# Straight-line stages, the slot transposes in the scores' bank, and the attention scores moved between the MLP tiles

## The chip, the cores and the metric

The kernel runs on one core of a Trainium2 chip. Its engines run in parallel, each with its own instruction stream in program order, and they wait for one another with semaphores: PE (TensorE, matrix products and transposes), ACT (ScalarE), DVE (VectorE), POOL (GpSimd) and SP (SyncE, which starts the DMAs). The metric is the device time of the program in microseconds.

## The reference: what is computed

Eight batch rows of 256 tokens with 256 features are normalised, and two branches are added to the input. The first is a gated slot attention with 16 heads and 64 slots:

```
A  = tril(q @ k.T) * scale                    # q, k after the rotary embedding
ok = enz * (A @ es)                           # es = exp(clip(s)), enz = 1 / cumsum(es) over tokens
qv = softmax(ok)                              # over the 64 slots
W2 = tril((qv * enz) @ es.T)
o  = W2 @ v
out = (o * rsqrt(mean(o*o) + eps) * g_norm * silu(g)) @ Wo.T
```

The second is an MLP with 2048 hidden units whose 4-bit weights are decoded on the chip: `out = (gelu(x @ Wg.T) * (x @ Wu.T)) @ Wd.T`. The result is x plus both branches, in fp32.

## The kernel before

The work is cut into 32 stages. Stage `st = 4 * hp + bp` handles pair `hp` of heads (two heads, eight pairs) and pair `bp` of batch rows (512 tokens, four pairs). With each pair of heads a stage also does one eighth of the MLP, in four tiles of 128 hidden units (`mlp_up` 0 to 3). The stages are pipelined: while a stage does its attention, PE projects v, gate, q and k for the next one (`project_vg`, `project_qk`), and it also does the output product of the one before (`outputs`).

The order on every engine is the order in which the code writes it; no scheduler moves anything. `each_stage` writes the first four stages and the last four out, and puts the 24 between them into a hardware loop of six rounds with four stages each. Each projection is three products in fp32r (high and low parts, lines 203 to 205); scores, values and transposes are plain fp32 products.

PE's order in a stage before is: `scores` for i = 0, 1 (first head, two batch rows; lines 292 and 294), `mlp_up` 0 and 1, `scores` 2 and 3 (second head), `mlp_up` 2 and 3, `gated_transpose` of the stage before (L349), `slot_scores` (L277), `project_vg` 0 and 1, `slot_reads`, `outputs` 0, `project_vg` 2, `slot_rows` (transposes of okz, L316), `outputs` 1, `project_vg` 3, the transposes of the softmax's result sm (L475), `project_qk` 0 and 1, `slot_weights` 0 (L324), `project_qk` 2 and 3, `slot_weights` 1, `values` 0, `slot_transpose` (four transposes of the next stage's es, L282) and `values` 1 (lines 338 to 341).

What surrounds these steps on the other engines:

- DVE masks each score matrix (`diagonal`, L740), and ACT copies its off-diagonal part (`off_diagonal`, L591). DVE also sums the squares of the stage before and POOL takes the power (L1092). DVE then multiplies by scale (L761) and gate (`gate_o`, L769), for which `gated_transpose` waits.
- The softmax over slots is `softmax_max` on DVE (L816), eight exponentials on ACT (`softmax_exp`, L586), the transposes L475 on PE, and `slot_query` on DVE.
- `copy_J` on ACT (L577) moves the transposed es out of its bank, for the next stage's `slot_reads`. It stands between the two squares of o (L597) at the end of a stage.
- For the next stage's q and k, `swap_halves` on ACT (L567, L568), `rope_cos` and `rope_sin` on DVE (L857, L860) and `rotate` on POOL (L1087) work in a chain with two buffers.

Two PSUM banks, `sc[0]` and `sc[1]`, hold all short-lived results of the attention. `sc_bank` gives eleven uses in a stage alternate banks, so that the roles change from stage to stage.

Of the kernel before, what the change touches and what calls it, by code (L numbers as in the profile page):

```python
# [37 lines left out]
P = 128  # L38
# [18 lines left out]
SC_SLOTS = {"A": (0, 1, 2, 3), "S": (4,), "K": (5,), "W": (6, 7, 8, 9), "E": (10,)}  # L57
SC_STEP = 11


def build(nc, x, w_qkvg, w_packed, w_scaled, w_slot, w_slot1, g_norm, rope_tab, out):
    with ExitStack() as ctx:
# [125 lines left out]
        def sc_bank(bp, kind, i=0):  # L188
            return sc[(SC_STEP * bp + SC_SLOTS[kind][i]) % 2]
# [21 lines left out]
        def _(sp):  # L211
# [12 lines left out]
            with sp.Fori(0, HP - 1) as hp:  # L224
# [15 lines left out]
        def _(pe):  # L240
# [32 lines left out]
            def slot_scores(n, bp, hp):  # L273

                if bp == 0:
                    pe.wait_ge(ws2_lo, 4 * hp + 4)
                pe.matmul(sc_bank((bp - 1) % BP, "S")[:, :] if n is not None else sc[1][:, :],  # L277
                          ws2[:, :], h1[:, bp, :], start=True, stop=True).then_inc(S_full, 1)
# [6 lines left out]
            def scores(st, bp, i, hp):  # L285
# [4 lines left out]
                dst = sc_bank(bp, "A", i)  # L290
# [20 lines left out]
            def slot_rows(st, bp):  # L311

                pe.wait_ge(okz_done, st + 1)
                dst = sc_bank(bp, "K")
# [4 lines left out]
            def slot_weights(st, bp, b):  # L319

                t0 = b * T
                pair = [(sc_bank(bp, "W", 2 * b + h), slice(h * M, (h + 1) * M)) for h in range(2)]
# [97 lines left out]
            def stage(hp, bp, first, last):  # L420
# [5 lines left out]

                for i in (0, 1):
                    if first and i == 1:
                        pe.wait_ge(clip_done, 1)
                    elif first or i == 1:  # L430
                        pe.wait_ge(J_ready, st + 1)
                    else:
                        pe.wait_ge(W_off, 4 * st)
# [29 lines left out]
                slot_rows(st, bp)  # L463
                if not first:
                    outputs(st, 1, php, st + 1)
                if not last:
# [48 lines left out]
        def _(act):  # L515
# [63 lines left out]
            def softmax_exp(st, bp):  # L579
# [3 lines left out]
                src = sc_bank(bp, "K")  # L583
# [5 lines left out]
            def off_diagonal(diag, done, dst, bp, kind, st, i, scale):  # L589
                act.wait_ge(diag, 4 * st + i + 1)  # L590
                act.activation(dst[i][:, 1, :], sc_bank(bp, kind, i)[:, P:2 * P], ACT.Copy,  # L591
# [68 lines left out]
            def stage(hp, bp, first, last):  # L660
                st = 4 * hp + bp
                npar = (bp + 1) % 2
                a_args = (A_diag, A_off, At, bp, "A", st)
                w_args = (W_diag, W_off, Wt, bp, "W", st)
                more = not (isinstance(hp, int) and hp == HP - 1)
# [28 lines left out]
                softmax_exp(st, bp)  # L694
# [24 lines left out]
                if not last:  # L719
                    copy_J(st + 1, sc_bank(bp, "E", 0)[:, :])  # L720
# [8 lines left out]
        def _(dve):  # L729
# [6 lines left out]
            def diagonal(full, done, dst, bp, kind, st, i, mask, used):  # L736
                dve.wait_ge(full, 4 * st + i + 1)
                wait(dve, *used)
                src = sc_bank(bp, kind, i)[:, 0:3 * P].rearrange("p (n t) -> p n t", n=3)
# [73 lines left out]
            def softmax_max(st, bp):  # L813
                dve.wait_ge(K_full, st + 1)
                wait(dve, p_ready, st)
                dve.tensor_reduce(mx[:, :], sc_bank(bp, "K")[:, :].rearrange("p (g m) -> p g m", m=M),  # L816
# [400 lines left out]
```

## Time and profile before

| | us |
|---|---|
| median of 3 runs | 1188.34 |
| lowest and highest | 1185.62, 1189.64 |
| profiled execution, its own time | 1186.13 |
| span of that execution | 1184.4 |
| PE busy | 1114.7 |
| DVE busy | 943.1 |
| ACT busy | 642.1 |
| POOL busy | 419.6 |

The span is the time from the first to the last instruction. Matmuls overlap in the records, so a stretch in which PE never waits is best read from start to start: 0.23 us from one full fp32r product of 512 columns to the next. The mean granted clock of PE was 0.986 of full speed. Stages begin, for instance, at 290.11 us (stage 7), 328.61 (stage 8), 362.78 (stage 9) and 397.07 (stage 10).

### The profile page before, as it was taken

The numbers are of one execution on the slowest core, as the hardware profiler recorded it, in microseconds if no ns is written. First come the engines' busy times: TensorE is split into PE (matmuls) and PEld (weight loads), VectorE is DVE, ScalarE is ACT, GpSimd is POOL, SyncE is SP. The second block draws the span as 40 slices with busy tenths as digits, with TensorE's granted clock in tenths as the row PEclk, the third lists the DMA queues.
The fourth block names the chain that finished last, engine by engine and source line by source line (L and its number), as shares of the span: only waits on it lengthen the run. The fifth ranks groups of instructions, "written<-read, shape, count | busy, mean of one in ns | idle before, by whom it ended". The sixth has DMA issues, their size and how long they took to land.

```text
span 1184.4 us, 20879 instructions
## 1 busy us (share of the span) xinstructions
PE 1114.7 (94%) x6872; PEld 941.6 (79%) x6872; DVE 943.1 (80%) x1808; ACT 642.1 (54%) x1748; POOL 419.6 (35%) x306
## 2 busy tenths in 40 slices
PE   6789999999999998999989999899998999999995
PEld 5568888888788887888878888788887888788884
DVE  6888887888868887888877888778886888877763
ACT  5355564655645565555655556464563565655451
POOL 5233242433513335232443324343251433523231
PEclk9899999999999999999999999999999999999998
DMA  4001000100001000010000100001000100000001
GB/s 157 1 1 74 1 1 1 52 22 1 1 2 73 1 1 2 1 73 1 1 3 1 74 1 1 3 16 59 1 1 2 73 1 1 1 2 19 1 19 36
DMA packets 9117, 23.19 MB, mean 20 GB/s; under 512 B 816, under 2 KB 5808, under 8 KB 7984
## 3 DMA queue, kind: packets, MB, share of 16 engines
q1 hardware_dynamic: 9008, 21.76, 5.0%
q8 instruction: 66, 1.08, 0.4%
q14 instruction: 43, 0.35, 0.1%
HBM read 19.66 MB, written 2.10 MB: 18 GB/s over the span
## 4 chain that ended last, share of the span: by engine, by line
PE 71%; issue 8%; DVE 6%; ACT 6%; POOL 3%; POOLq 0%; DVEq 0%; ACTq 0%
PE bank L203 17%; PE bank L205 16%; PE bank L204 16%; PE bank L292 5%; ACT xs L568 3%; PE bank L305 3%; PE bank L349 2%; DVE xs L860 2%; POOL qkT L1087 2%; PE bank L294 2%; DVE Wt L740 2%; ACT xs L567 2%; PE bank L282 1%; PE bank L338 1%; PE bank L341 1%
## 5 line engine op out<-in xcount | busy, mean ns | idle before, releaser
L1096 POOL TENSOR_TENSOR inter_lo<-ffb,inter_hi 128x512 fp32r<-128x512 f32 x64 | 83.3, 1323 | 433.2 <-ACT inter_hi L617 433.2
L1087 POOL TENSOR_TENSOR qkT<-ra,xs 128x512 f32<-128x512 f32 x128 | 163.5, 1277 | 95.1 <-DVE xs L860 67.6
L586 ACT ACTIVATE sm<-bank,mx 128x64 f32<-128x64 f32 x256 | 76.3, 325 | 168.5 <-DVE mx L816 168.5
L857 DVE TENSOR_TENSOR ra<-bank,rope 128x512 f32<-128x512 f32 x128 | 88.0, 687 | 55.1 <-ACT xs L568 54.9
L805 DVE RECIPROCAL enzT<-enzT 128x256 f32<-128x256 f32 x64 | 111.6, 1744 | 0.0
L860 DVE TENSOR_TENSOR xs<-xs,rope 128x512 f32<-128x512 f32 x128 | 109.0, 852 | 0.0
L203 PE MATMUL bank<-xh,wqk_hi 128*128 128x512 f32 x256 | 107.4, 420 | 0.0
L203 PE MATMUL bank<-xh,wgu_hi 128*128 128x512 f32 x256 | 106.9, 418 | 0.0
L591 ACT ACTIVATE At<-bank 128x128 f32<-128x128 f32 x128 | 35.4, 276 | 132.0 <-DVE At L740 132.0
L205 PE MATMUL bank<-xh,wgu_lo 128*128 128x512 f32 x256 | 101.6, 397 | 0.0
L203 PE MATMUL bank<-wvg_hi,xh 128*128 128x512 f32 x256 | 101.4, 396 | 0.0
L204 PE MATMUL bank<-xl,wgu_hi 128*128 128x512 f32 x256 | 101.1, 395 | 0.0
L204 PE MATMUL bank<-wvg_lo,xh 128*128 128x512 f32 x256 | 101.0, 395 | 0.0
L205 PE MATMUL bank<-wvg_hi,xl 128*128 128x512 f32 x256 | 101.0, 395 | 0.0
L205 PE MATMUL bank<-xh,wqk_lo 128*128 128x512 f32 x256 | 100.8, 394 | 0.0
L204 PE MATMUL bank<-xl,wqk_hi 128*128 128x512 f32 x256 | 100.1, 391 | 0.0
L567 ACT ACTIVATE xs<-bank 64x512 f32<-64x512 f32 x128 | 76.1, 595 | 42.8 <-POOL qkT L1087 33.7
L292 PE MATMUL bank<-qkT 128*128 128x256 f32 x256 | 79.3, 392 | 14.1 <-issue 9.7
L1092 POOL TENSOR_TENSOR rstd<-mse,mhalf 128x8 f32<-128x8 f32 x32 | 52.7, 1647 | 91.4 <-DVE mse L756 91.4
L740 DVE TENSOR_TENSOR At<-bank,mask_a 128x256 f32<-128x256 f32 x128 | 53.4, 418 | 33.8 <-PE bank L294 33.5
L203 PE MATMUL bank<-wod_hi,ogT_hi 128*128 128x256 f32 x256 | 78.8, 308 | 1.5 <-ACT ogT_hi L602 1.5
L568 ACT ACTIVATE xs<-bank 64x512 f32<-64x512 f32 x128 | 75.5, 590 | 1.5
(137 smaller groups left out, 3211.5 us busy)
## 6 DMA issues: line engine op xcount, KB each, us to landing
raw<-in_w_qkvg SPq DMA_DIRECT2D x8, 1024.0 KB, 4.9
scaled<-in_w_scaled SPq DMA_DIRECT2D x8, 640.0 KB, 7.7
packed<-in_w_packed SPq DMA_DIRECT2D x8, 384.0 KB, 5.4
acc<-in_x SPq DMA_DIRECT2D x4, 512.0 KB, 8.6
out<-acc SPq DMA_DIRECT2D x4, 512.0 KB, 3.0
ws_raw<-in_w_slot SPq DMA_DIRECT2D x8, 48.0 KB, 1.8
rope<-in_rope_tab SPq DMA_DIRECT2D x1, 256.0 KB, 7.0
osq<-in_w_slot SPq DMA_DIRECT2D x1, 128.0 KB, 3.3
```

The lines of the kernel that those rows point to most:

```text
L203: pe.matmul(dst, stat[0], mov[0], start=start, stop=False)
L204: pe.matmul(dst, stat[0], mov[1], start=False, stop=False)
L205: return pe.matmul(dst, stat[1], mov[0], start=False, stop=stop)
L292: pe.matmul(dst[:, 0:T], qkT[:, 2 * h + 1, t0:t0 + P], qkT[:, 2 * h, t0:t0 + T], start=True, stop=True)
L567: act.activation(xs[i % 2][0:64, :], pj[i][64:128, :], ACT.Copy)
L568: act.activation(xs[i % 2][64:128, :], pj[i][0:64, :], ACT.Copy).then_inc(swapped, 1)
L740: dve.tensor_tensor(dst[i][:, 0:3:2, :], src[:, 0:3:2, :], mask[:, :, :], ALU.mult).then_inc(done, 1)
L805: dve.reciprocal(enzT[par][:, c], enzT[par][:, c]).then_inc(enz_ready, 1)
L857: dve.tensor_tensor(two(ra[i % 2][:, :]), two(pj[i][:, :]), cos, ALU.mult).then_inc(cos_done, 1)
L860: dve.tensor_tensor(two(xs[i % 2][:, :]), two(xs[i % 2][:, :]), sin, ALU.mult).then_inc(sin_done, 1)
L1087: pool.tensor_tensor(qkT[:, i, :], ra[i % 2][:, :], xs[i % 2][:, :], ALU.add).then_inc(roped, 1)
L1096: pool.tensor_tensor(inter[1][e][:, :], ffb[e][:, :], inter[0][e][:, :].bitcast(F32), ALU.subtract).then_inc(inter_lo, 1)
```

## The change

It has four parts.

1. All 32 stages are written out; the hardware loop goes on every engine that had it.
2. `sc_bank` goes. Scores and weights use `sc[0]` for the one of a pair and `sc[1]` for the other, the slot scores S and the es transposes use `sc[0]`, and the okz transposes use `sc[1]`, in every stage.
3. `slot_transpose` moves on PE from between the two `values` to between `outputs` 1 and `project_vg` 3. `copy_J` moves on ACT from behind the first square of o to ahead of `softmax_exp`. `slot_weights` 0 now waits for `copy_J`.
4. On PE `scores` 0 and 1 move behind `mlp_up` 0, and `scores` 2 and 3 behind `mlp_up` 2.

```diff
         def each_stage(eng, stage):
-            for bp in range(BP):
-                stage(0, bp, bp == 0, False)
-            with eng.Fori(1, HP - 1) as hp:
-                for bp in range(BP):
-                    stage(hp, bp, False, False)
-            for bp in range(BP):
-                stage(HP - 1, bp, False, bp == BP - 1)
+            for hp in range(HP):
+                for bp in range(BP):
+                    stage(hp, bp, hp == bp == 0, hp == HP - 1 and bp == BP - 1)
...
+                mlp_up(st, bp, hp, 0)
                 for i in (0, 1):
...
                     scores(st, bp, i, hp)
-                mlp_up(st, bp, hp, 0)
                 mlp_up(st, bp, hp, 1)
+                mlp_up(st, bp, hp, 2)
                 for i in (2, 3):
                     pe.wait_ge(A_off, 4 * st + i - 1)
                     scores(st, bp, i, hp)
-                mlp_up(st, bp, hp, 2)
                 mlp_up(st, bp, hp, 3)
...
                     outputs(st, 1, php, st + 1)
+                if not last:
+                    pe.wait_ge(es_ready, st + 2)
+                    slot_transpose(sc[0], esT[nbp % 2])
                 if not last:
                     project_vg(st + 1, nbp, nhp, 3, True)
...
                 pe.wait_ge(qe_ready, st + 1)
-                pe.wait_ge(A_off, 4 * st + 4)
-                if not last:
-                    pe.wait_ge(clip_done, st + 2)
+                if not last:
+                    pe.wait_ge(J_ready, st + 2)
                 slot_weights(st, bp, 0)
...
                 values(st, bp, 0)
-                if not last:
-                    pe.wait_ge(es_ready, st + 2)
-                    pe.wait_ge(W_off, 4 * st + 3)
-                    slot_transpose(sc_bank(bp, "E", 0), esT[nbp % 2])
...
# ScalarE
-                softmax_exp(st, bp)
+                if not last:
+                    copy_J(st + 1, sc[0][:, :])
+                softmax_exp(st)
...
                 square_o(st, 0)
-                if not last:
-                    copy_J(st + 1, sc_bank(bp, "E", 0)[:, :])
                 square_o(st, 1)
```

The next rows are the instruction order as the two programs issue it; the square brackets name the semaphores that a row waits for. First PE, ahead of the transposes of sm, before: the last `project_vg` tile (wvg) stands directly behind `outputs` 1 (wod).

```order
L205 MATMUL bank<-wod_hi,inter_lo 128x256
L203 MATMUL bank<-wvg_hi,xh 128x512 [waits inter_done]
L204 MATMUL bank<-wvg_lo,xh 128x512
L205 MATMUL bank<-wvg_hi,xl 128x512
L203 MATMUL bank<-wvg_hi,xh 128x512
L204 MATMUL bank<-wvg_lo,xh 128x512
L205 MATMUL bank<-wvg_hi,xl 128x512
L475 MATMUL bank<-ident,sm 128x128 [waits acc_done,p_ready]
```

The same place after the change, where the es transposes stand between them (L273 is L282 of before, and L467 is L475):

```order
L196 MATMUL bank<-wod_hi,inter_lo 128x256
L273 MATMUL bank<-ident,esT 128x128 [waits es_ready]
L273 MATMUL bank<-ident,esT 128x128 x3
L194 MATMUL bank<-wvg_hi,xh 128x512 [waits inter_done]
L195 MATMUL bank<-wvg_lo,xh 128x512
L196 MATMUL bank<-wvg_hi,xl 128x512
L194 MATMUL bank<-wvg_hi,xh 128x512
L195 MATMUL bank<-wvg_lo,xh 128x512
L196 MATMUL bank<-wvg_hi,xl 128x512
L467 MATMUL bank<-ident,sm 128x128 [waits acc_done,p_ready]
```

Four transposes have come in between, and the transposes of sm still wait for the exponentials (p_ready). Second ACT, in the middle of a stage, before: the exponentials of the softmax follow the first two copies of v and tanh of the gate.

```order
L559 ACTIVATE vS<-bank 128x256 [waits vg_full]
L561 ACTIVATE th<-bank 128x256 [waits G_ready]
L586 ACTIVATE sm,ssum<-bank,mx 128x64 [waits rs_done,pT_full,mx_done]
L586 ACTIVATE sm,ssum<-bank,mx 128x64 x7
L559 ACTIVATE vS<-bank 128x256 [waits vg_full]
```

The same place after the change, with the copy of the transposed es to esJ (`copy_J`):

```order
L546 ACTIVATE vS<-bank 128x256 [waits vg_full]
L548 ACTIVATE th<-bank 128x256 [waits G_ready]
L564 ACTIVATE esJ<-bank 128x512 [waits ok_full,E_full]
L573 ACTIVATE sm,ssum<-bank,mx 128x64 [waits rs_done,pT_full,mx_done]
L573 ACTIVATE sm,ssum<-bank,mx 128x64 x7
L546 ACTIVATE vS<-bank 128x256 [waits vg_full]
```

The exponentials now stand behind a copy that waits for the es transposes on PE (E_full). Third PE, at the end of a stage and the start of the next, before (the six products of values 0 stand ahead of these rows):

```order
L282 MATMUL bank<-ident,esT 128x128 [waits W_off,es_ready]
L282 MATMUL bank<-ident,esT 128x128 x3
L338 MATMUL bank<-vS,Wt 128x128 [waits W_off]
L340 MATMUL bank<-vS,Wt 128x128
L341 MATMUL bank<-vS,Wt 128x128
L338 MATMUL bank<-vS,Wt 128x128
L340 MATMUL bank<-vS,Wt 128x128
L341 MATMUL bank<-vS,Wt 128x128
L292 MATMUL bank<-qkT 128x256 [waits roped,W_off]
L294 MATMUL bank<-qkT 128x128
L292 MATMUL bank<-qkT 128x256 [waits J_ready]
L294 MATMUL bank<-qkT 128x128
```

The same place after the change (L332 is L341, and L283 is L292; wgu is the MLP tile):

```order
L329 MATMUL bank<-vS,Wt 128x128 [waits W_off]
...
L332 MATMUL bank<-vS,Wt 128x128
L194 MATMUL bank<-xh,wgu_hi 128x512 [waits cos_done,w_lo]
L195 MATMUL bank<-xl,wgu_hi 128x512
L196 MATMUL bank<-xh,wgu_lo 128x512
L194 MATMUL bank<-xh,wgu_hi 128x512
L195 MATMUL bank<-xl,wgu_hi 128x512
L196 MATMUL bank<-xh,wgu_lo 128x512
L283 MATMUL bank<-qkT 128x256 [waits roped,W_off]
L285 MATMUL bank<-qkT 128x128
L283 MATMUL bank<-qkT 128x256 [waits W_off]
L285 MATMUL bank<-qkT 128x128
```

The es transposes are gone from here, values 1 keeps its own wait for W_off, and one MLP tile now stands between the values and the first scores.

## Rows read from the trace of the kernel before

**Rows 1.** Page, part 1: busy us (share of the span) xinstructions.

```profile
PE 1114.7 (94%) x6872; PEld 941.6 (79%) x6872; DVE 943.1 (80%) x1808; ACT 642.1 (54%) x1748; POOL 419.6 (35%) x306
```

**Rows 2.** Waits of PE: waiting line, releaser, us in total, times, longest us.

```profile
PE bank L282 <- ACT Wt L591: 20.2, 27, 2.1
...
PE bank L292 <- issue: 9.7, 5, 2.5
```

**Rows 3.** Windows, the five fourth stages before a jump back (span, busy, PEclk).

```profile
290.11:328.61 38.50, 35.56 (x215) 30.09 (x214) 30.83 (x56) 23.39 (x59) 19.74 (x13) 0.96 0.01 2
...
sum 192.00, PE 171.77 PEld 144.78 DVE 154.09 ACT 116.91 POOL 98.65; mean PE 34.35 PEld 28.96 DVE 30.82 ACT 23.38 POOL 19.73
```

**Rows 4.** Windows: stages 8, 16, 27 (left by the loop's end), 28 (written out).

```profile
328.61:362.78 34.17, 33.98 (x213) 28.81 (x214) 26.58 (x53) 17.82 (x51) 8.82 (x7) 1.00 0.01 2
610.46:646.25 35.79, 35.60 (x214) 30.05 (x214) 26.68 (x53) 17.82 (x51) 8.82 (x7) 0.95 0.01 2
998.01:1033.99 35.98, 33.88 (x216) 28.70 (x215) 30.80 (x56) 22.78 (x58) 18.98 (x13) 1.00 0.00 1
1033.99:1068.30 34.31, 33.89 (x216) 28.70 (x214) 27.03 (x53) 18.41 (x52) 9.58 (x8) 1.00 0.01 2
```

**Rows 5.** Timeline, softmax of stage 8: start us, us, engine, line, tiles.

```profile
347.92 0.31 ACT L586 ACTIVATE sm<-bank,mx 128x64 f32<-128x64 f32 x1 [6.36 <-DVE mx L816]
...
349.84 0.40 PE L203 MATMUL bank<-wvg_hi,xh 128*128 128x512 f32 x1
...
351.23 0.60 PE L475 MATMUL bank<-ident,sm 128*128 128x128 f32 x4
...
351.58 0.47 PE L203 MATMUL bank<-xh,wqk_hi 128*128 128x512 f32 x1
...
353.25 0.59 ACT L567 ACTIVATE xs<-bank 64x512 f32<-64x512 f32 x1
```

**Rows 6.** Timeline, softmax of stage 0.

```profile
60.85 0.31 ACT L586 ACTIVATE sm<-bank,mx 128x64 f32<-128x64 f32 x1 [3.68 <-DVE mx L816]
...
63.38 0.66 PE L475 MATMUL bank<-ident,sm 128*128 128x128 f32 x4 [2.55 <-ACT sm L586]
...
65.48 0.59 ACT L567 ACTIVATE xs<-bank 64x512 f32<-64x512 f32 x1
```

**Rows 7.** Timeline, es transposes and their copy at the end of stage 8.

```profile
360.55 0.45 ACT L591 ACTIVATE Wt<-bank 128x128 f32<-128x128 f32 x2
...
360.97 0.63 PE L282 MATMUL bank<-ident,esT 128*128 128x128 f32 x4 [0.19 <-ACT Wt L591]
...
361.64 0.60 ACT L577 ACTIVATE esJ<-bank 128x512 f32<-128x512 f32 x1 [0.15 <-PE bank L282]
```

**Rows 8.** Timeline, end of stage 7 (a fourth stage).

```profile
320.60 2.35 POOL L1066 TENSOR_TENSOR wgu_lo<-raw,wgu_hi 128x1024 fp32r<-128x1024 f32 x1
...
321.03 2.47 DVE L860 TENSOR_TENSOR xs<-xs,rope 128x512 f32<-128x512 f32 x1
...
324.29 0.95 PE L282 MATMUL bank<-ident,esT 128*128 128x128 f32 x4 [2.12 <-ACT Wt L591]
```

**Rows 9.** Timeline, starts of stages 9 and 10 up to the gated transposes.

```profile
362.78 0.60 PE L292 MATMUL bank<-qkT 128*128 128x256 f32 x2
...
363.64 0.42 DVE L740 TENSOR_TENSOR At<-bank,mask_a 128x256 f32<-128x256 f32 x1 [1.19 <-PE bank L294]
...
367.03 0.69 DVE L761 TENSOR_TENSOR scal<-rstd,rs 128x8 f32<-128x8 f32 x1
...
370.94 0.60 PE L349 MATMUL bank<-ident,og 128*128 128x128 f32 x4
...
398.28 0.41 DVE L740 TENSOR_TENSOR At<-bank,mask_a 128x256 f32<-128x256 f32 x1
...
403.24 1.12 DVE L769 SCALAR_TENSOR_TENSOR og<-bank,scal,G 128x128 f32<-128x128 f32 x4
```

**Rows 10.** Timeline, the decoding step behind `slot_query` in stage 9.

```profile
387.25 1.23 DVE L867 TENSOR_SCALAR packed<-packed 128x768 int32<-128x768 int32 x1
```

More of the change, by code:

```diff
@@ L223, in _ @@
                     sp.dma_start(scaled[:, :], w_scaled[0]).then_inc(scaled_in, 16)
-            with sp.Fori(0, HP - 1) as hp:
+            for hp in range(HP - 1):
                 sp.wait_ge(w_lo, 4 * hp + 4)
@@ L276, in slot_scores @@
                     pe.wait_ge(ws2_lo, 4 * hp + 4)
[L277 removed]
+                pe.matmul(sc[0][:, :] if n is not None else sc[1][:, :],
                           ws2[:, :], h1[:, bp, :], start=True, stop=True).then_inc(S_full, 1)
@@ L321, in slot_weights @@
                 t0 = b * T
-                pair = [(sc_bank(bp, "W", 2 * b + h), slice(h * M, (h + 1) * M)) for h in range(2)]
+                pair = [(sc[h], slice(h * M, (h + 1) * M)) for h in range(2)]
                 for dst, g in pair:
@@ L424, in stage @@
                 php = hp - 1 if bp == 0 else hp
+                mlp_up(st, bp, hp, 0)
                 for i in (0, 1):
[L428 to L431, printed above, removed]
+                    if first:
+                        pe.wait_ge(clip_done if i == 1 else J_ready, 1)
                     else:
-                        pe.wait_ge(W_off, 4 * st)
+                        pe.wait_ge(W_off, 4 * st - 1 + i)
                     scores(st, bp, i, hp)
-                mlp_up(st, bp, hp, 0)
                 mlp_up(st, bp, hp, 1)
+                mlp_up(st, bp, hp, 2)
                 for i in (2, 3):
@@ L587, in softmax_exp, with off_diagonal @@
                 ins.then_inc(p_ready, 1)
-            def off_diagonal(diag, done, dst, bp, kind, st, i, scale):
+            def off_diagonal(diag, done, dst, st, i, scale):
                 act.wait_ge(diag, 4 * st + i + 1)
-                act.activation(dst[i][:, 1, :], sc_bank(bp, kind, i)[:, P:2 * P], ACT.Copy,
+                act.activation(dst[i][:, 1, :], sc[i % 2][:, P:2 * P], ACT.Copy,
                                scale=scale).then_inc(done, 1)
@@ L662, in stage @@
                 npar = (bp + 1) % 2
-                a_args = (A_diag, A_off, At, bp, "A", st)
-                w_args = (W_diag, W_off, Wt, bp, "W", st)
-                more = not (isinstance(hp, int) and hp == HP - 1)
+                a_args = (A_diag, A_off, At, st)
+                w_args = (W_diag, W_off, Wt, st)
+                more = hp < HP - 1
                 off_diagonal(*a_args, 0, SCALE)
@@ L734, in two, with diagonal @@
                 return ap.rearrange("p (b t) -> p b t", b=2)
-            def diagonal(full, done, dst, bp, kind, st, i, mask, used):
+            def diagonal(full, done, dst, st, i, mask, used):
                 dve.wait_ge(full, 4 * st + i + 1)
                 wait(dve, *used)
-                src = sc_bank(bp, kind, i)[:, 0:3 * P].rearrange("p (n t) -> p n t", n=3)
+                src = sc[i % 2][:, 0:3 * P].rearrange("p (n t) -> p n t", n=3)
                 dve.tensor_tensor(dst[i][:, 0:3:2, :], src[:, 0:3:2, :], mask[:, :, :], ALU.mult).then_inc(done, 1)
@@ L946, in stage @@
                 par, npar, pbp = bp % 2, (bp + 1) % 2, (bp - 1) % BP
-                more = not (isinstance(hp, int) and hp == HP - 1)
-                a_args = (A_full, A_diag, At, bp, "A", st)
-                w_args = (W_full, W_diag, Wt, bp, "W", st)
+                more = hp < HP - 1
+                a_args = (A_full, A_diag, At, st)
+                w_args = (W_full, W_diag, Wt, st)
                 if bp == 3 and more:
@@ L1135, in stage @@
                 st = 4 * hp + bp
-                more = not (isinstance(hp, int) and hp == HP - 1)
+                more = hp < HP - 1
                 if first:
```

24 lines of the change are left out of this document (10 added, 14 removed).

## The prediction

> **What bounds the kernel now.** I read the page first. PE is busy for 94% of the span and the next engine, DVE, for 80% [rows 1]. So PE's own order is the clock of the kernel, and other engines matter only where PE waits. The chain that ended last says the same. The waits of PE come next. Apart from the start and the end of the program, only two groups count: 20.2 us ahead of the es transposes, where PE waits for ACT's copy of the masked weights, and 9.7 us ahead of the first scores, five times, with no releaser that the profile shows [rows 2]. The five times are the five jumps back of the loop. The windows by stage show what they cost: the fourth stages ahead of a jump last 192.0 us together [rows 3], the one that leaves the loop without a jump 35.98 us [rows 4]. The reader is to see two more things there. A stage in the loop and a written-out one take the same time (34.17 and 34.31 us, granted clock 1.00), so the loop costs nothing between its jumps. And a stage with a stretch at 1.2 GHz instead of 2.4 GHz (granted clock 0.95) takes 35.79 us instead of 34.17, which is 1.62 us more [rows 4].
>
> **1. Written-out stages: a gain of 15.3 us.** Five fourth stages give back 192.0 - 5 x 35.98 = 12.1 us. Two of the stages behind a jump were lengthened by the slow clock that its wait left behind, 2 x 1.62 = 3.2 us (one of the two is in [rows 4]). The sum is 15.3 us, of which 9.7 us is the wait itself [rows 2]. The Trainium skill ("Runtime: NRT & Kernel Launch", "Instruction fetch mechanics") states that prefetch of instructions is sequential and that a taken branch to a page that isn't held stalls the engine until it is fetched. The trace agrees, since the wait stands only at the jumps. By that rule the gain is whole; if the 9.7 us had another source that stays, the time would be some 15 us above my sum.
>
> **2. The copy ahead of the exponentials: a new wait of 2.0 us in each stage.** This is the term that decides. Call e the start of the es transposes in their new place, which is where `project_vg` 3 started before (349.84). PE then needs 0.35 us for four transposes (as L475, 351.23 to 351.58), 1.39 us for `project_vg` 3 (349.84 to 351.23), and 0.07 us more for its first product, since one behind a plain fp32 product takes 0.47 us instead of 0.40 [rows 5]. It stands before the transposes of sm at e + 1.8. ACT can start `copy_J` 0.67 us after the first es transpose (360.97 to 361.64), and it takes 0.60 us [rows 7], so the exponentials start at e + 1.28. Before, they started at 347.92, when DVE's maximum came, 1.9 us ahead of e; so their input now lies ready for 3.2 us. From the first exponential to the transposes of sm there are 2.53 us, as stage 0 shows, where PE really waited for them [rows 6]. So PE goes on at e + 3.8 instead of e + 1.8. That is 1.99 us of waiting. The slack that hid the exponentials before was 351.23 - (347.92 + 2.53) = 0.78 us, and they are moved by 3.2 us against `outputs` 1. The whole difference lies on PE's path, since there is no other instruction for PE to take. Thirty stages have both `outputs` 1 and a next stage: 30 x 1.99 = 59.7 us. Behind that wait ACT has its two copies of v, two tanh and two splits before `swap_halves`: it started 2.02 us after L475 before (351.23 to 353.25) and 2.10 us where PE had waited (63.38 to 65.48) [rows 5, 6]. So 0.08 us is lost there, and nothing is caught up.
>
> **3. The scores behind an MLP tile: a wait for the gate of 0.2 to 0.7 us.** `gated_transpose` started 8.16 us after the stage did (362.78 to 370.94). DVE's first mask came 0.86 us after the first score [rows 9]. Now the first score comes 1.46 us later (one MLP tile, 1.39 + 0.07), so the mask starts at 2.32. DVE does the sum of squares, the norm and the gate in that order behind it, and ends 6.08 us after it started (398.28 to 403.24 + 1.12) [rows 9]: 8.40 us. PE arrives at 8.16 + 0.07 = 8.23, the 0.07 being one more change from fp32 to fp32r. That makes 0.2 us of waiting in second-batch-pair and later stages, a little more (0.3) in first ones. In the second stage of each four, the multiplication by scale, an operation on eight columns, takes 0.69 us beside POOL's decoding [rows 9]; I add 0.5 us for it, which gives 0.7 us. Seven first stages at 0.3, eight second at 0.7, eight third and seven fourth at 0.2 make 10.7 us, and the last stage, which has no projections to fill the time, 1.5 us: 12.2 us. Bounds: nothing, if DVE finds the same waits elsewhere shorter, and 1.46 us x 31 = 45 us, if all of the shift showed; the rows speak for the low part.
>
> **4. The wait ahead of the es transposes doesn't go with them.** `values` 1 has a wait of its own, for the second of the two copies of which the es transposes waited for the first. The two end 0.17 us apart (0.45 us for two of 0.28) [rows 7]. So PE waits at `values` 1 for what it waited for at L282, and 0.17 us longer, and 0.08 us longer by the lateness in part 2. In the second stages the decoding step of 1.23 us [rows 10] stands on DVE between `slot_query` and the rotary part. What follows the exponentials comes 0.78 us later against PE (the slack of part 2 that is gone), and so does this step; I take it that 0.2 us of that is absorbed: 0.6 us more. Per four stages this is 4 x 0.25 + 0.6 = 1.6 us, over 7.75 fours 12.4 us. The wait of 2.12 us in fourth stages stays: DVE's `rope_sin` there takes 2.47 us beside POOL's split of the MLP weights and ends 0.55 us after it [rows 8]. The Trainium skill ("SBUF — State Buffer", "SBUF: two separate sides") states that VectorE and GpSimd share one port pair under an exclusive lock, and that the later one is blocked for the whole instruction. The rows agree; by that rule the wait can't be had by moving PE's transposes.
>
> **5. Small terms.** The es transposes cost PE 0.42 us in the new place (0.35 + 0.07), and about as much before; with the change from fp32 at the stage's start (0.07) I count 0.05 us a stage, 1.6 us. The banks' new roles add the wait of `slot_weights` 0 for `copy_J`, which ends at e + 1.3, while `slot_weights` 0 comes behind two projections more; nothing. `copy_J` no longer stands between the squares of o; ACT is idle there, so nothing is gained. The DMAs keep their places.
>
> **6. The clock.** Of the five jumps, each with two waits near 2 us within five us, three left a stretch at 1.2 GHz (granted clock 0.96 and 0.95 [rows 3, 4], and once more like the latter). That is 3 of 10 waits. Thirty new waits of 2.0 us would give 9 such stretches of 1.62 us, 14.6 us; about a third comes back, since the later wait at `values` 1 gets shorter where PE is slower ahead of it. I take 9 us. The bounds are 0 and 30 x 1.62 = 49 us.
>
> **Sum.** 59.7 + 12.2 + 12.4 + 1.6 + 9 - 15.3 = 79.6 us. The rows come from an execution of 1186.1 us in its own time, span 1184.4, which lies 2.2 us below the median of the runs. 1188.3 + 79.6 gives **1268 us**.
>
> **The rivals.**
> - Only the wait for the exponentials shows; the gate and the values' waits come out as before, and the clock stays at full speed. 1188.3 + 59.7 + 1.6 - 15.3 = 1234 us. For it: DVE and ACT idle for a fifth and more of the span [rows 1], and some of it may be in the right place. Against it: the chain of part 3 has 8.16 - 0.86 - 6.08 = 1.2 us of slack and is moved by 1.46. Chance 0.17.
> - The slow clock comes after nearly every new wait: 1268 - 9 + 49 = 1308 us. For it: the waits are as long as those that led to it. Against it: seven in ten of those didn't. Chance 0.14.
> - The other side: the exponentials are not late. They would be hidden if the path from the first es transpose to their end fitted in 1.8 us instead of 3.8, or if their input came that late already. Then parts 2 and 6 fall away, and if PE's wait of 20.2 us also went with the transposes, the time would be 1188.3 - 20.2 - 15.3 + 1.6 = 1154 us. The point that decides is e + 1.8. Every piece of the 3.8 us is a row, so I give this 0.03.
> - Writing the stages out costs elsewhere: the longer program is fetched once in place of a loop. Stages 28 to 31 are such code already and 28 shows no wait but that at L282 [rows 4]. The gain of part 1 would be lost: 1268 + 15 = 1283 us. Chance 0.05.
> - The forecast itself, within 1248 to 1288: 0.6. The last 0.01 is for no change.
>
> **Range and chances.** From between the first rival and the forecast up to between the forecast and the second: 1240 to 1296 us. A measurement here can tell about 0.3%, that is 4 us. Faster than that 0.04, within it 0.01, slower 0.95.
>
> **What the profile after would show.** Right: a wait of PE of about 2.0 us at L467 for ACT's exponentials (L573), some thirty times, 60 us in total; a wait of 0.2 to 0.7 us at L340 for DVE; a wait at the first product of the second `values` (L329) for ACT, 0.4 us in most stages and 2.3 in fourth ones; no wait without a releaser at the stage starts; stages of some 37 us and fourth ones near 39. Wrong: exponentials that start before the es transposes, or no wait at L467. If the waits are as told and the time is not, the clock's stretches are miscounted, which the windows would show.

## The result and the profile after

The changed kernel takes 1262.81 us (median of 4 runs, 1262.2 to 1263.69) against 1186.98 us before (1185.38 to 1189.64). The ratio is 1.0637, with a 95% interval of 1.0613 to 1.0661. It is slower by 6.4%. The prediction said 1268 us, with a range of 1240 to 1296 us: the median is inside the range and 5 us below the forecast. The profiled execution has a span of 1261.9 us, 77.5 us more than before.

First the page of the kernel after, its busy times (to compare with [rows 1]):

```profile
PE 1136.9 (90%) x6872; PEld 943.2 (75%) x6872; DVE 942.1 (75%) x1808; ACT 629.6 (50%) x1748; POOL 421.0 (33%) x306
```

The numbers of instructions on the engines are the same, and PE is busy for a smaller share. So the time went into PE's waits. Its waits by releaser, of the kernel after (total us, times, longest; to compare with [rows 2]):

```profile
PE bank L467 <- ACT sm L573: 52.4, 32, 2.1
PE bank L329 <- ACT Wt L578: 26.4, 30, 2.7
...
PE bank L340 <- DVE og L756: 10.6, 10, 5.9
PE bank L194 <- POOL wgu_lo L1053: 5.4, 1, 5.4
```

The five waits at the jumps are gone. The wait for the exponentials stands first, with 32 times, and the wait for ACT's copies of the weights has not gone with the es transposes: it was 20.2 us at L282 and is 26.4 us at the second `values`. The page's list understates such waits, since the modelled end of a matmul reaches over the start of the idle time. What PE really loses is better read from start to start. The timeline of stage 9 after, at the moved transposes (to compare with [rows 5]):

```profile
406.20 0.60 PE L307 MATMUL bank<-ident,okz 128*128 128x128 f32 x4
406.83 0.69 DVE L803 TENSOR_REDUCE mx<-bank 128x8 f32<-128x512 f32 x1 [0.80 <-PE bank L307]
...
409.47 0.60 PE L273 MATMUL bank<-ident,esT 128*128 128x128 f32 x4
...
410.11 0.60 ACT L564 ACTIVATE esJ<-bank 128x512 f32<-128x512 f32 x1 [8.32 <-PE bank L273]
410.60 0.31 ACT L573 ACTIVATE sm<-bank,mx 128x64 f32<-128x64 f32 x1
...
413.13 0.66 PE L467 MATMUL bank<-ident,sm 128*128 128x128 f32 x4 [1.66 <-ACT sm L573]
```

DVE has the maximum at 407.52. ACT has been idle for 8.32 us and does not start the exponentials, because `copy_J` stands ahead of them and waits for transposes that PE issues at 409.47. From there 0.64 us go by to the copy, 0.49 us to the first exponential, 2.53 us to the transposes of sm: 3.66 us, of which PE fills 1.82. It loses 1.84 us, in every one of 30 stages (3.66 us from L273 to L467 in each of them).

The windows of four stages after (stages 8 to 11: span, busy, granted clock; to compare with [rows 4]):

```profile
349.64:387.46 37.82, 35.77 (x216) 29.60 (x215) 26.67 (x53) 17.88 (x52) 9.20 (x8) 0.96 0.00 1
387.46:424.72 37.26, 34.43 (x216) 28.58 (x215) 28.07 (x56) 18.83 (x53) 13.39 (x11) 1.00 0.16 58
424.72:461.14 36.42, 34.41 (x217) 28.58 (x215) 28.79 (x57) 18.07 (x53) 9.31 (x8) 1.00 0.00 1
461.14:499.93 38.79, 34.72 (x216) 28.85 (x215) 30.89 (x57) 22.38 (x58) 19.56 (x13) 0.99 0.01 1
sum 150.29, PE 139.34 PEld 115.61 DVE 114.43 ACT 77.16 POOL 51.46; mean PE 34.84 PEld 28.90 DVE 28.61 ACT 19.29 POOL 12.86
```

The same four stages took 140.69 us before (328.61 to 469.30), so four stages have grown by 9.6 us, although the 2.1 us that the jump at 469.30 cost are gone. Around the start of each first stage of a four (here at 349.64) lies a stretch at 1.2 GHz. The timeline of the kernel after around one, the end of stage 11, shows where it begins:

```profile
498.29 0.49 PE L329 MATMUL bank<-vS,Wt 128*128 128x128 f32 x2 [2.38 <-ACT Wt L578]
...
499.06 0.39 PE L329 MATMUL bank<-vS,Wt 128*128 128x128 f32 x2
...
499.64 0.63 PE L332 MATMUL bank<-vS,Wt 128*128 128x128 f32 x2
499.93 0.77 PE L194 MATMUL bank<-xh,wgu_hi 128*128 128x512 f32 x1
500.50 0.63 PE L195 MATMUL bank<-xl,wgu_hi 128*128 128x512 f32 x1
```

PE waits 2.4 us at the second `values`, starts at full speed, and 1.1 us later the clock falls: each product then takes 0.43 us from start to start instead of 0.23. This comes after each of the seven such waits of fourth stages, and after none of the thirty waits for the exponentials. Before there were four such stretches between the first stage and the last, two after waits of fourth stages and two after jumps.

The gate's wait at `gated_transpose` is the third one. (Its longest, 5.9 us, is that of the last stage, which was there before with 6.0 us.) Stage 9 after, the second of a four, on PE (to compare with [rows 9]):

```profile
395.49 0.40 PE L196 MATMUL bank<-xh,wgu_lo 128*128 128x512 f32 x1
396.44 1.09 PE L340 MATMUL bank<-ident,og 128*128 128x128 f32 x8 [0.55 <-DVE og L756]
```

And stage 10, the third:

```profile
432.73 0.40 PE L196 MATMUL bank<-xh,wgu_lo 128*128 128x512 f32 x1
433.18 1.09 PE L340 MATMUL bank<-ident,og 128*128 128x128 f32 x8
```

The next instruction would start 0.23 us after the last one, so PE loses 0.72 us in the second stage of a four, and 0.22 us in the third, where the list of waits has nothing at all. In the first and the fourth it loses 0.24 and 0.20 us by the same reading: 1.4 us in four stages.

### The profile page after: what moved, and what is told of

Its sections match the earlier page's. It is cut to its first block, busy times and chain, and to the rows that moved or that the text cites. A ratio compares the mean times of both kernels' runs of the same rounds, so it can differ in the third digit from the quotient of the medians.

```text
span 1261.9 us, 19839 instructions
## 1 busy us (share of the span) xinstructions
PE 1136.9 (90%) x6872; PEld 943.2 (75%) x6872; DVE 942.1 (75%) x1808; ACT 629.6 (50%) x1748; POOL 421.0 (33%) x306
## 4 chain that ended last, share of the span: by engine, by line
PE 46%; ACT 17%; issue 14%; DVE 13%; POOL 4%; POOLq 0%; DVEq 0%; ACTq 0%
PE bank L194 11%; PE bank L195 10%; PE bank L196 10%; ACT sm L573 6%; DVE Wt L727 3%; DVE og L756 3%; POOL rstd L1079 3%; PE bank L340 3%; ACT xs L554 3%; ACT xs L555 3%; PE bank L296 2%; DVE xs L847 2%; ACT inter_hi L604 2%; PE bank L283 2%; DVE ra L844 1%
## 5 line engine op out<-in xcount | busy, mean ns | idle before, releaser
L777 DVE SCALAR_TENSOR_TENSOR G<-th,bank 128x256 f32<-128x256 f32 x128 | 52.4, 410 | 110.6 <-ACT th L548 110.6
L564 ACT ACTIVATE esJ<-bank 128x512 f32<-128x512 f32 x32 | 19.2, 599 | 220.0 <-PE bank L273 219.9
L194 PE MATMUL bank<-xh,wgu_hi 128*128 128x512 f32 x256 | 112.9, 441 | 5.4 <-POOL wgu_lo L1053 5.4
L847 DVE TENSOR_TENSOR xs<-xs,rope 128x512 f32<-128x512 f32 x128 | 112.0, 875 | 0.0
L196 PE MATMUL bank<-xh,wgu_lo 128*128 128x512 f32 x256 | 104.3, 408 | 0.0
L194 PE MATMUL bank<-wvg_hi,xh 128*128 128x512 f32 x256 | 104.3, 408 | 0.0
L195 PE MATMUL bank<-xl,wgu_hi 128*128 128x512 f32 x256 | 103.9, 406 | 0.0
L554 ACT ACTIVATE xs<-bank 64x512 f32<-64x512 f32 x128 | 76.3, 596 | 40.8 <-POOL qkT L1074 34.0
L329 PE MATMUL bank<-vS,Wt 128*128 128x128 f32 x256 | 57.3, 307 | 27.5 <-ACT Wt L578 26.4
```

The source lines that it names most:

```text
L194: pe.matmul(dst, stat[0], mov[0], start=start, stop=False)
L195: pe.matmul(dst, stat[0], mov[1], start=False, stop=False)
L196: return pe.matmul(dst, stat[1], mov[0], start=False, stop=stop)
L554: act.activation(xs[i % 2][0:64, :], pj[i][64:128, :], ACT.Copy)
L847: dve.tensor_tensor(two(xs[i % 2][:, :]), two(xs[i % 2][:, :]), sin, ALU.mult).then_inc(sin_done, 1)
```

## The experiments

Twelve kernels ran, in three groups of four; each was timed against the kernel before (1186.7 to 1186.8 us in these groups). Spans, waits and stretches are those of one profiled execution of each. "Slow stretches" are those at 1.2 GHz between the starts of stage 1 and stage 31. Their number can differ between executions of one kernel: the mean granted clock of the kernel before was 0.978 to 0.986, that of the changed kernel 0.979 to 0.982.

### First group: one part undone, or one part alone

**copy_behind_exp.** The changed kernel, with the copy behind the exponentials:

```diff
-                if not last:
-                    copy_J(st + 1, sc[0][:, :])
                 softmax_exp(st)
+                if not last:
+                    copy_J(st + 1, sc[0][:, :])
```

> The changed kernel with one edit: the copy of the transposed es stands behind the eight exponentials on ACT; the transposes on PE keep their new place. Theory (the exponentials wait for the copy, the copy for PE): they start again when DVE's maximum comes, PE's wait for them, 1.84 us in each of 30 stages, goes, and 55 us come back: 1208 us (1200 to 1216). Rival (the loss comes from the scores' place or from the banks' roles): above 1250 us, and the wait of PE for the exponentials turns up as another wait.

Measured: 1198.98 us, ratio 1.0097 (1.0079 to 1.0116); span 1197.5 us. Its waits of PE:

```profile
PE bank L329 <- ACT Wt L578: 23.0, 30, 2.5
...
PE bank L467 <- ACT sm L573: 2.6, 2, 2.1
```

Of 32 waits for the exponentials two are left, those of the first and the last stage. 64 us came back with two lines moved. That is more than the 55 us of the waits: there are three slow stretches instead of seven, 4 x 1.62 = 6.5 us, and the waits at L329 are 3.4 us less. The expectation (1200 to 1216 us) had counted the waits alone and was just missed.

**es_ahead_of_outputs.** The changed kernel, with the es transposes ahead of `outputs` 1 on PE and the copy left where the change put it:

```diff
                 slot_rows(st)
+                if not last:
+                    pe.wait_ge(es_ready, st + 2)
+                    slot_transpose(sc[0], esT[nbp % 2])
                 if not first:
                     outputs(st, 1, php, st + 1)
-                if not last:
-                    pe.wait_ge(es_ready, st + 2)
-                    slot_transpose(sc[0], esT[nbp % 2])
```

> The changed kernel with the es transposes directly behind the okz transposes on PE, ahead of the output product; the copy stays ahead of the exponentials on ACT. The copy can then start 1.0 us behind the first okz transpose and the exponentials 1.5 us behind it, where DVE's maximum came 1.4 us behind it before. Theory (what costs is only that the copy waits for transposes behind the output product): as with the copy behind the exponentials, 1208 us (1200 to 1216). Rival (the copy ahead of the exponentials costs its own 0.6 us of PE time wherever it waits): 1226 us.

Measured: 1199.91 us, ratio 1.0104 (1.0085 to 1.0123); span 1198.3, with four slow stretches. Here, too, only two of the waits for the exponentials are left:

```profile
PE bank L467 <- ACT sm L573: 2.6, 2, 2.1
```

The two cures are worth the same. So neither place brings the wait by itself: the copy may stand ahead of the exponentials if the transposes come early, and the transposes may come late if the copy stands behind. Only the pair costs the 1.84 us a stage. (The late transposes have a smaller price of their own; see halves_es_moved.)

**loop_out_only.** The kernel before with `each_stage` and SP's loop written out as in the change, nothing else.

> The kernel before with only the loop written out on all engines. Theory (the jumps cost 12.1 us and leave the slow clock twice): 1187 - 15.3 = 1172 us (1168 to 1177), no wait without a releaser at the stages' starts, and the waits at the es transposes as before, 20 us. Rival (the wait at the jumps has another source, or the longer program costs as much): 1187 us.

Measured: 1182.79 us, ratio 0.9965 (0.9952 to 0.9979). It is faster, by 4 us and not by 15. The waits at the jumps are gone, as expected. But the windows over the slow stretches in this kernel's trace show seven of them instead of four, one after each wait of fourth stages (three of the seven rows):

```profile
186.50:189.90 3.40, 3.35 (x16) 3.38 (x17) 1.81 (x3) 1.32 (x3) 1.94 (x2) 0.52 0.01 2
326.40:329.80 3.40, 3.40 (x17) 3.40 (x18) 1.75 (x3) 1.26 (x3) 1.88 (x2) 0.53 0.00 0
...
1026.10:1029.50 3.40, 3.40 (x18) 3.31 (x18) 1.61 (x3) 1.34 (x4) 1.72 (x2) 0.54 0.00 0
```

The sum is 12.1 us back, 3 x 1.62 = 4.9 us lost, 2.3 us lost ahead of stage 1 (see the last section), and 1.6 us lost in the last stage, where slow stretches also lie: 3.3 us back, which is the difference of the spans (1184.4 and 1181.1). The medians differ by 4.0.

The 12.1 us are the right total and the wrong parts. They were read from fourth stages [rows 3], and stage 7 among these took its 38.50 us with a wait of only 1.1 us at the jump and 1.4 us of slow clock. From start to start the five waits at the jumps add up to 10.6 us. Against loop_out_only, PE's waits at the es transposes inside the loop are 1.4 us longer, about 0.08 us each in first, third and fourth stages. So the loop did cost a little between its jumps.

My expectation (1168 to 1177 us) had the slow clock as a debt of the jumps alone. It isn't: the wait of 2 us in fourth stages, which the loop had as well, can bring it.

**scores_back.** The changed kernel with both pairs of scores back in their old places.

```diff
-                mlp_up(st, bp, hp, 0)
                 for i in (0, 1):
...
+                mlp_up(st, bp, hp, 0)
                 mlp_up(st, bp, hp, 1)
-                mlp_up(st, bp, hp, 2)
                 for i in (2, 3):
...
+                mlp_up(st, bp, hp, 2)
                 mlp_up(st, bp, hp, 3)
```

> The changed kernel with the scores back in their old places, ahead of MLP tiles 0 and 2. Theory: the waits of PE for the gate (0.2 to 0.7 us a stage, 11 us in all), one change of precision a stage (about 2 us) and 2 us in stage 0 go: 1248 us (1242 to 1254), with the wait for the exponentials still at 1.84 us a stage. Rival (the scores' place costs nothing, the loss is all of the exponentials): 1262 us. Rival (most of the loss is of the scores): below 1225 us.

Measured: 1238.96 us, ratio 1.0443 (1.0421 to 1.0465); span 1236.5. PE's waits for the gate are gone but for the last:

```profile
PE bank L467 <- ACT sm L573: 52.0, 32, 2.1
PE bank L329 <- ACT Wt L578: 26.3, 30, 2.7
...
PE bank L340 <- DVE og L756: 6.0, 1, 6.0
```

The span is 25.4 us shorter than the changed kernel's, 10 us more than expected. There is one slow stretch here instead of seven, which is 6 x 1.62 = 9.7 us. What is left for the scores' place is 15.7 us. The waits of fourth stages are as long as in the changed kernel (2.38 us in both lists), and here six of the seven did not bring the slow clock.

### Second group: the clock, the sum, and a larger dose

**two_undone.** The changed kernel with both of the edits above, copy_behind_exp and scores_back.

> The changed kernel with two edits undone: the scores stand where they stood, and the copy of es follows the exponentials on ACT. What is left of the change is the written-out stages, the banks' new roles and the es transposes ahead of the last value projection. Theory (the two edits make up the loss, and their costs add): the span of the kernel with the copy behind, 1197.5 us with three stretches of slow clock of 1.62 us, less 15.7 us for the scores, is 1177 us with none and 1188 us with seven. Rival (the costs overlap): 1195 us or more.

Measured: 1183.23 us, ratio 0.9971 (0.9961 to 0.9981); span 1181.6, with three slow stretches. 1177 + 3 x 1.62 is 1181.9. The costs add.

**split_in_halves.** The kernel of loop_out_only, and on POOL:

```diff
+            def split_half(hp, k):
+                if k == 0:
+                    pool.wait_ge(w_hi, 4 * hp + W_GU + 1)
+                ins = pool.tensor_tensor(wgu[1][:, k, :], mlp_raw[:, k, :], wgu[0][:, k, :].bitcast(F32), ALU.subtract)
+                if k == 1:
+                    ins.then_inc(w_lo, 1)
...
-                        if i == 1 and bp == 3 and more:
-                            split_lo(hp + 1, W_GU)
+                        if i in (1, 2) and bp == 3 and more:
+                            split_half(hp + 1, i - 1)
```

> The kernel before with the loop written out, and POOL's split of the MLP weights cut into two halves, one behind the second rotation and one behind the third, so that DVE's sine product in fourth stages waits for one half only. Theory (the 2 us wait of PE in fourth stages comes from that product, held up by POOL, and this wait brings the slow clock seven times): the wait falls from 2.0 to about 0.9 us, 7.7 us come back, and with the seven slow stretches 11 us more: 1182.8 - 19 = 1164 us. Rival (the wait has another cause): 1183 us. Rival (the wait falls but the slow clock stays): 1175 us.

Measured: 1162.5 us, ratio 0.9791 (0.9776 to 0.9807). The end of stage 7 in this kernel's timeline (to compare with [rows 8]):

```profile
321.50 1.28 POOL L1067 TENSOR_TENSOR wgu_lo<-raw,wgu_hi 128x512 fp32r<-128x512 f32 x1
...
321.94 1.38 DVE L856 TENSOR_TENSOR xs<-xs,rope 128x512 f32<-128x512 f32 x1
...
324.12 0.63 PE L278 MATMUL bank<-ident,esT 128*128 128x128 f32 x4 [0.96 <-ACT Wt L587]
```

DVE's sine product takes 1.38 us instead of 2.47, PE's wait is 0.96 instead of 2.02 us, and no slow stretch is left between the first stage and the last. 7 x 1.06 + 7 x 1.62 = 18.8 us; the span is 19.6 us shorter (1161.5 against 1181.1 in loop_out_only).

**split_halves_in_loop.** The same cut in the kernel before, with its loop.

> The same cut of POOL's split in the kernel before, with its loop kept. Theory: 7.7 us of waiting come back and up to 4 slow stretches (6.5 us), the jumps stay: 1186.8 - 8 to - 14 = 1173 to 1179 us; and the written-out kernel with the same cut is 10 to 12 us below this one. Rival (written-out stages gain nothing once the clock is out of the way): both within 3 us.

Measured: 1177.07 us, ratio 0.9919 (0.99 to 0.9938); span 1174.0, one slow stretch, which begins during a wait at a jump. With the clock nearly out of the way, the written-out stages are worth 14.6 us between the medians of this kernel and the last one, 12.5 us between the spans (10 to 12 us were expected). The list of waits names POOL's rotation as the releaser of the waits at the jumps here (five of the six in this row; the other, of 4.0 us, is in stage 0):

```profile
PE bank L292 <- POOL qkT L1094: 14.7, 6, 4.0
```

The five are 2.0 to 2.3 us each, where the kernel before had 0.8 to 2.5 us. The second rotation, for which PE waits there, is long done (behind stage 11 at 457.37, where PE goes on at 464.15), so I read them as the same waits. That a jump makes PE wait is shown, since the waits go with the loop; what PE waits for at a jump no run shows.

**second_copy.** The changed kernel, with one more copy on ACT ahead of `copy_J`'s, from the same bank into a tile `pad` that nobody reads.

```diff
                 wait(act, ok_full, n)
+                if n > 0:
+                    wait(act, pad_done, n - 1)
+                    act.activation(pad[:, :], src, ACT.Copy).then_inc(pad_done, 1)
                 act.activation(esJ[:, :, :].rearrange("p n m -> p (n m)"), src, ACT.Copy).then_inc(J_ready, 1)
```

> The changed kernel with one more copy of 512 columns on ACT ahead of the copy of es, into a tile that nobody reads. Theory (ACT's chain from the es transposes to the exponentials is PE's path): each of 30 stages gets 0.61 us longer at the wait for the exponentials, 18 us, before what the clock does: 1281 us, or 1270 to 1295 with the clock's changes. Rival (some other limit sets the stage's length): 1263 us.

Measured: 1291.52 us, ratio 1.0885 (1.0865 to 1.0906); span 1289.4. Its waits of PE:

```profile
PE bank L469 <- ACT sm L578: 66.6, 32, 2.1
PE bank L331 <- ACT Wt L583: 24.1, 28, 2.5
```

Each wait for the exponentials grew by 0.47 us (from 1.66 to 2.13 in the list), 30 x 0.47 = 14.1 us; two copies in a row take that, not the 0.61 us that I used. There are fourteen slow stretches instead of seven, and 7 x 1.62 = 11.3 us. Together 25.4 of the 27.5 us; the rest was not followed up. The seven new stretches come after the waits for the exponentials, now 2.3 us from start to start.

### Third group: each part on ground without slow stretches

The first three put parts of the change, or all of it, into the kernel of split_in_halves (span 1161.5), so that the clock does not blur them. In all three no slow stretch is left between stages 1 and 31.

**halves_scores_moved.** That kernel with the two pairs of scores moved as in the change.

> The written-out kernel with POOL's split in halves (1162.5 us, no slow stretch between the first and the last stage), and in it the scores' move alone. Theory (the move costs PE's waits for the gate, 1.4 us in four stages, a change of precision in each, and 2 to 3 us in stage 0): 1162.5 + 11 + 2 + 2 = 1177 us (1172 to 1181). Rival (15 us was the slow clock's doing): 1164 us.

Measured: 1185.13 us, ratio 0.9987 (0.9974 to 1.0001); span 1181.9, so 20.4 us for the move, 5 us more than expected. Its waits:

```profile
PE bank L345 <- DVE og L765: 10.6, 10, 6.0
PE bank L278 <- ACT Wt L587: 9.4, 14, 0.9
PE bank L199 <- POOL wgu_lo L1062: 6.2, 1, 6.2
...
PE bank L199 <- POOL wgu_lo L1067: 2.7, 7, 0.4
```

The last row is a wait that the two edits make together: with an MLP tile at the head of a stage, PE needs the second half of the split at once, 0.55 us from start to start, 7 times: 4 us. Without it the move costs 16.5 us, as scores_back showed from the other side (15.7). The waits for the gate are 11 to 12 us of that. The rest is about 0.07 us a stage for one more change between fp32 and fp32r, and a longer stage 0 (POOL's split at L199, 6.2 us).

**halves_es_moved.** That kernel with the new roles of the banks and the es transposes in their new place, the copy behind the exponentials.

> The written-out kernel with POOL's split in halves, the banks' new roles and the es transposes in their new place, with the copy behind the exponentials and the scores in their old places. Theory (what is left of the change costs little; PE waits at the second values for the second copy instead of the first): 1162.5 + 7 = 1169.5 us (1166 to 1173). Rival (banks and transposes are free): 1162.5 us.

Measured: 1168.37 us, ratio 0.9841 (0.9812 to 0.9869); span 1167.8. What is left of the change costs 6.3 us:

```profile
PE bank L329 <- ACT Wt L578: 15.2, 30, 1.2
```

It was 9.6 us in 14 waits at the es transposes. PE comes to the second `values` a little earlier, needs the second copy instead of the first, and waits. The new roles of the banks and the new place of the transposes were not tried apart, so the 6.3 us are for both.

**halves_whole_change.** The changed kernel with the split in halves.

> The changed kernel with POOL's split in halves. Theory (the slow clock in it follows the wait of fourth stages only, seven times, and never the wait of 1.84 us for the exponentials): the wait of fourth stages gets 1.1 us shorter, 7.5 us, and seven slow stretches go, 11.3 us: 1262.8 - 19 = 1244 us. Rival (the slow clock moves to the waits for the exponentials): 1255 us or more.

Measured: 1251.65 us, ratio 1.0549 (1.0517 to 1.0582); span 1247.2. Its waits for the exponentials and for the split's second half:

```profile
PE bank L467 <- ACT sm L573: 52.1, 32, 2.1
...
PE bank L194 <- POOL wgu_lo L1058: 3.5, 7, 0.5
```

The waits for the exponentials are the same, and no slow stretch follows any of them, so the rival is refuted for this execution. The 14.7 us that came back between the spans are the 18.8 us of split_in_halves, less 4 to 5 us of waiting for the second half, which the expectation (1244 us) had left out. The profiled execution is the fastest of the four; between the medians 11.2 us came back.

On this ground, without slow stretches, the whole change costs 1247.2 - 1161.5 = 85.7 us: 20.4 for the scores, 6.3 for banks and transposes, and 59.0 that are left for the copy ahead of the exponentials, whose waits are 55.2.

**masks_before_sine.** The kernel of split_in_halves, and on DVE:

```diff
                     rope_cos(st + 1, 2)
-                    rope_sin(st + 1, 2)
                 diagonal(*w_args, 2, mask_w, (o_full, 2 * st))
                 diagonal(*w_args, 3, mask_w, (o_full, 2 * st))
                 if not last:
+                    rope_sin(st + 1, 2)
```

> The written-out kernel with POOL's split in halves, and on DVE the two last weight masks ahead of the third sine product instead of behind it. Theory (PE's waits of 0.36 to 1.1 us at the es transposes are for those masks, which stand behind 0.6 to 1.4 us of sine product): most of 2.4 us in four stages goes, 13 us or a little more: 1149 us (1145 to 1155). Rival (the later third and fourth rotations then hold up the second head's scores or the next stage): 1160 us or more.

Measured: 1158.77 us, ratio 0.9764 (0.9739 to 0.9789); span 1157.0. It is the fastest of all, but 4.5 us of the span came back and not 13. The timeline of its stage 9 shows what took the place of the sine product:

```profile
388.68 0.75 DVE L736 TENSOR_TENSOR Wt<-bank,mask_w 128x256 f32<-128x256 f32 x2
388.80 0.59 ACT L563 ACTIVATE xs<-bank 64x512 f32<-64x512 f32 x1 [0.76 <-POOL qkT L1090]
...
389.40 0.59 ACT L564 ACTIVATE xs<-bank 64x512 f32<-64x512 f32 x1
...
390.01 0.45 ACT L587 ACTIVATE Wt<-bank 128x128 f32<-128x128 f32 x2
...
390.44 0.63 PE L278 MATMUL bank<-ident,esT 128*128 128x128 f32 x4 [0.41 <-ACT Wt L587]
```

DVE's masks are done at 389.43, but ACT does the last `swap_halves` first, until 389.99. PE's wait in second stages is still 0.41 us. Only in fourth stages, where the sine product was long, did the masks' place matter. Moving ACT's copies ahead of that swap was not tried.

## Why the prediction was right, step by step

The step that decides, the second, was right in mechanism and in size. The total is nearer than the parts, and that is luck: against the 77.5 us between the spans, steps 2, 4 and 6 were 4.5, 7.0 and 0.9 us too large, and step 5 and a loss ahead of stage 1 that the prediction didn't have were 4.0 and 4.8 us too small.

- **Step 2, the exponentials behind the copy: right.** 1.99 us a stage and 59.7 us were predicted, 1.84 us and 55.2 us were measured. The bound was built from single durations, and two of them were a little long: 0.67 + 0.60 us up to the first exponential, where 0.64 + 0.49 us passed, since a short operation on ACT starts before a 512-column copy has ended by its record. The mechanism is shown by three runs: copy_behind_exp and es_ahead_of_outputs take it away in two ways, second_copy enlarges it.
- **Step 3, the scores and the gate: right.** Predicted 0.2 to 0.7 us a stage, 12.2 us in all; measured 1.4 us in four stages, 10.9 us, and 1.0 us more in the last stage (L296 waits 2.0 us there instead of 1.02). scores_back removes it. The move as a whole costs 15.7 to 16.5 us, with what it adds in stage 0 and at changes of precision.
- **Step 4, the wait that doesn't go with the transposes: right in kind, too large.** Predicted 12.4 us more; measured, from start to start, 0.7 us more in four stages, 5.4 us. The term for the decoding step failed: I had it 0.6 us late in every second stage, but it took 0.64 us after instead of 1.23 [rows 10], and so made good what it was late (the row stands below the list). The 0.25 us for each stage came out as 0.11 in first and third stages, 0.21 in second and 0.27 in fourth ones.
- **Step 1, the written-out stages: the waits right, the clock wrong.** 12.1 us came back, though not all of it at the jumps (10.6 us there; see loop_out_only). The two slow stretches behind jumps went too, as credited (3.2 us), but the written-out stages brought five others, after waits of fourth stages, so that the clock costs more and not less.
- **Step 6, the clock: nearly the right size for the wrong reason.** I had nine new stretches after the waits for the exponentials, and two fewer from the jumps, together 5.8 us. There were none after those waits. The two after jumps went, and there were five more after the waits of fourth stages (seven of seven instead of two): three more in all, 4.9 us. The rival in which the slow clock follows nearly every wait is refuted for waits of 1.84 us; in second_copy, at 2.3 us, seven did bring it.
- **Step 5, the small terms: too small.** In stage 9 PE's start-to-start times outside the waits grew by 0.18 us, not 0.05: about 0.09 at the stage's start, 0.08 behind the es transposes, 0.06 more in each of two restarts after a new wait, less what the es transposes cost among the values. 31 x 0.18 = 5.6 us instead of 1.6.
- **Not in the prediction:** stage 1 begins 4.75 us later (at 86.59 instead of 81.84). 2.5 us of it are the start of the program, below; the rest is stage 0, whose first MLP tile waits for POOL's split (5.4 us where PE had waited 3.9 us for the rotation), and which has 3.4 us more at 1.2 GHz.

The row of step 4, the decoding step in stage 9 after (to compare with [rows 10]):

```profile
415.84 0.64 DVE L854 TENSOR_SCALAR packed<-packed 128x768 int32<-128x768 int32 x1
```

Step by step the sum is 55.2 + 10.9 + 1.0 + 5.4 + 5.6 + 4.9 + 4.8 - 12.1 = 75.7 us of 77.5. What remains, 1.8 us, I can't place.

The rival of the other side needed exponentials that end by e + 1.8; they end at e + 3.7. The one in which only their wait shows fell with the gate's waits.

## What to carry to other kernels

Before a copy is put ahead of a chain on an in-order engine, look at what the copy waits for and not at what it costs: 0.6 us of work held up exponentials whose input had been ready for 3 us, because its source came later in another engine's order. Follow the wait, too: a transpose that is moved away from a wait leaves the wait to the next instruction that needs the same thing. And when waits of about 2 us stand in a TensorE stream, count the stretches at 1.2 GHz in each trace before a difference of 1% is put down to an edit: here they moved results by 5 to 11 us in kernels whose waits were about equally long, and shortening the one wait paid twice.

## What the hardware showed unexpectedly

**The same wait may or may not bring the slow clock.** The waits of fourth stages at the second `values` or the es transposes are 2.0 to 2.7 us long in each of these kernels. In the profiled executions they were followed by a stretch at 1.2 GHz 7 times in 7 in the changed kernel, in loop_out_only and in second_copy, 4 in 7 in es_ahead_of_outputs, 3 in 7 in copy_behind_exp and in two_undone, 2 in 7 in the kernel before, and once in 7 in scores_back. In two_undone it came after every second of these waits (stages 7, 15 and 23), in copy_behind_exp after those of stages 3, 11 and 19. What decides was not tried by itself. In split_in_halves and the four kernels built on it, where these waits are at most 1.3 us long, there was none.

**A transfer that lands earlier can cost time.** In all the written-out kernels PE gets its first normalised rows 2.5 to 3.1 us later (12.0 to 12.6 us instead of 9.5). In the first 13 us DVE normalises these rows, in the changed kernel for 3.92 us:

```profile
7.90 3.92 DVE L885 TENSOR_SCALAR og<-acc,mv,rstd 128x256 f32<-128x256 f32 x4 [1.14 <-POOL rstd L1106]
```

and POOL's first split of the weights begins within it:

```profile
9.01 2.34 POOL L1053 TENSOR_TENSOR wvg_lo<-raw,wvg_hi 128x1024 fp32r<-128x1024 f32 x1 [0.45 <-ACT wvg_hi L522]
```

In the kernel before, POOL's first split came later, because ACT had waited 4.3 us for the weights' DMA:

```profile
7.56 1.78 DVE L898 TENSOR_SCALAR og<-acc,mv,rstd 128x256 f32<-128x256 f32 x4 [1.14 <-POOL rstd L1119]
...
10.59 2.35 POOL L1066 TENSOR_TENSOR wvg_lo<-raw,wvg_hi 128x1024 fp32r<-128x1024 f32 x1 [2.37 <-ACT wvg_hi L535]
```

There the group on DVE was done before the split began; in the changed kernel the split begins inside it. The same two cases separate all the kernels: 3.80 to 3.94 us on DVE in the twelve with written-out stages, 1.78 us in the two with the loop. I read it as the same contention as in [rows 8]; no run moved the split by itself. Why the weights land earlier in the written-out kernels is open.
